# Latent-key attention: the causal mask added by VectorE in PSUM, in place of bf16 products of TensorE

## The chip, the core and the metric

The kernel runs on one core of a Trainium2 chip. It is written engine by engine: TensorE multiplies matrices into PSUM, VectorE and ScalarE read and write PSUM and SBUF, GpSimd works on SBUF, and semaphores order them. The metric is the device time of one execution in microseconds, the median of several runs.

## The reference

Eight layers are added one after another onto x of shape (4, 512, 256). Only the first concerns us, an attention with 16 heads and causal mask over 512 rows:

```python
q = (x @ wq).reshape(b, s, H, DN + DR)
q_nope, q_pe = (q[..., :DN], q[..., DN:])
q_pe = apply_rope(q_pe, cos, sin)
kv_a = x @ wkv_a
kv, k_pe = (kv_a[..., :R], kv_a[..., R:])
...
scores = jnp.einsum('bshd,bthd->bhst', qf, kf) * SCALE
mask = jnp.tril(jnp.ones((s, s), bool))
scores = jnp.where(mask[None, None], scores, jnp.finfo(scores.dtype).min)
p = jax.nn.softmax(scores, axis=-1)
out = jnp.einsum('bhst,bthd->bshd', p, v).reshape(b, s, H * DV)
return out @ wo
```

After it come a feed-forward layer, a cosine-similarity attention, the same feed-forward layer, a gated linear attention, a workspace layer, an attention with adapters and the workspace layer again.

## The kernel before

The latent-key attention is `mla_attention`. It folds the key weights into the queries, so that a head's key and query both have 128 rows (64 latent, 64 rotated). It loops over 32 pairs of heads, `n` = 0 to 31: 4 batches `b` of 8 pairs `p`. Head `j` of the pair is 0 or 1. The pairs are numbered 0 to 31 below.

There is no scheduler: each engine has its own list of calls, written out by hand, and semaphores between them. The scores of a head are a causal triangle of 128-wide tiles: tile row `qi` has (qi+1) x 128 columns. They lie in PSUM in `sc[:, j]`, three banks a head: row 3 in the first (512 columns), rows 2 and 0 in the second (384 + 128), row 1 in the third (256). `CAUSAL_ORDER` is 3, 2, 0, 1. `s_ready` counts finished banks.

The order of TensorE in pair n: `scores(n, 0)`, `spread_sums(n - 1)` (the reciprocal sums of the pair before, turned into `po`), `project(n + 1, 1)` (the rotated part of the next queries, into `pq`), `scores(n, 1)`, `attend(n - 1)` (probabilities times values, into `po`), `project(n + 1, 0)`, then `turn_probs` for both heads (ten transposes each), and pieces of row work for the next batch and the next layer ("lead" work), put in at certain pairs.

The order of VectorE: `maxima(n, 0)` (row maxima, negated, L535), `rope_queries(n + 1)`, `maxima(n, 1)`, `normalise(n - 1)` (onT), `copy_turned(n, 0)`, the reciprocal of the sums, `copy_turned(n, 1)`, and after that row and lead work, which stands ahead of `maxima(n + 1, 0)`.

The order of ScalarE: `exponents(n, 0)` (L681, for which it waits on `max_ready`), `copy_sums(n - 1)` (L674, `po` to `rb`), `exponents(n, 1)`, copies of the queries, and its share of the turned probabilities. `attend(n - 1)` waits for `r_copied`, that is for `copy_sums(n - 1)`; `turn_probs(n, j)` waits for the exponents of head j. GpSimd does the rotation (`rope`) and widens the reciprocal sums.

The mask on the diagonal tiles (0 below, -1e30 above the diagonal) is added by TensorE: behind each score product follows one of the identity with the mask tile, both in bf16, which accumulates into the diagonal tile (L792). float32 products show two passes in the trace, each with a weight load of its own.

Of the kernel before, what the change touches and what calls it, by code (L numbers as in the profile page):

```python
# [9 lines left out]
ALU = mybir.AluOpType  # L10
# [4 lines left out]
P = 128  # L15
B, S, D = 4, 512, 256
# [9 lines left out]
CAUSAL_COL = {3: 0, 2: S, 0: S + 3 * P, 1: 2 * S}  # L26
CAUSAL_COLS = 2 * S + 2 * P
CAUSAL_BANK = {3: 0, 2: 1, 0: 1, 1: 2}


class Kit:
# [339 lines left out]
def mla_attention(nc, g, w):  # L371


    with ExitStack() as ctx:
        k = Kit(nc, ctx)
        x, wap, wvo, ident, ident_b, mask_b = (g[n] for n in ("x", "wap", "wvo", "ident", "ident_b", "mask_b"))
# [13 lines left out]
        kT = k.sb("kT", [P, 2, 2, S])  # L390
        qT = k.sb("qT", [P, 2, 2, S])
# [30 lines left out]
        sc = k.ps("sc", [P, 2, 3 * 512])  # L422
# [16 lines left out]
        with nc.Block() as block:  # L439
# [15 lines left out]
            def _(dve):  # L455
# [74 lines left out]
                def maxima(n, j):  # L530
                    for qi in CAUSAL_ORDER:
                        if qi != 0:
                            dve.wait_ge(s["s_ready"], 6 * n + 3 * j + CAUSAL_BANK[qi] + 1)
                        at = CAUSAL_COL[qi]
                        red = dve.tensor_reduce(nmax[:, j, qi:qi + 1], sc[:, j, at:at + (qi + 1) * P],  # L535
                                                AX.X, ALU.max, negate=True)
                        if qi != 2:
                            red.then_inc(s["max_ready"], 1)
# [33 lines left out]
                for n in range(PAIRS):  # L572
                    b, p = divmod(n, MLA_PAIRS)
                    maxima(n, 0)
                    if n + 1 < PAIRS:
                        rope_queries(n + 1)
                    maxima(n, 1)
                    if n > 0:
                        normalise(n - 1)
                    copy_turned(n, 0)  # L580
                    if p == 6 and b + 1 < B:
                        scale_keys(b + 1)
                    dve.wait_ge(s["e_ready"], 6 * n + 6)
                    dve.reciprocal(rl[:, :, :], lsum[:, :, :]).then_inc(s["rl_ready"], 1)
                    copy_turned(n, 1)
                    if p == 0 and b > 0:
                        add_output(b - 1)
                    if b + 1 < B:
                        if p == 1:
                            row_stats(b + 1)  # L590
                        if p == 2:
                            norm_rows(b + 1)
                        if p == 5:
                            keys_values(b + 1, pq[:, :])
                    lead_vector(b, p)
# [52 lines left out]
            def _(act):  # L648
# [27 lines left out]
                def exponents(n, j):  # L676
                    for qi in CAUSAL_ORDER:
                        if qi != 0:
                            act.wait_ge(s["max_ready"], 6 * n + 3 * j + CAUSAL_BANK[qi] + 1)
                        at = CAUSAL_COL[qi]  # L680
# [40 lines left out]
            def _(pe):  # L721
# [57 lines left out]
                def scores(n, j):  # L779
                    b = n // MLA_PAIRS  # L780
                    if n > 0:
                        pe.wait_ge(s["pt_a"], 2 * (n - 1) + j + 1)
                        pe.wait_ge(s["pt_b"], 2 * (n - 1) + j + 1)
                    if j == 0:
                        pe.wait_ge(s["kT_ready"], 2 * b + 2)
                        pe.wait_ge(s["rope_done"], n + 1)
                        pe.wait_ge(s["qa_copied"], n + 1)
                    for qi in CAUSAL_ORDER:
                        at = CAUSAL_COL[qi]
                        pe.matmul(sc[:, j, at:at + (qi + 1) * P], qT[:, n % 2, j, qi * P:(qi + 1) * P],  # L790
                                  kT[:, b % 2, j, 0:(qi + 1) * P], start=True, stop=False)
                        last = pe.matmul(sc[:, j, at + qi * P:at + (qi + 1) * P], ident_b[:, :], mask_b[:, :],  # L792
                                         start=False, stop=True)
                        if qi != 2:
                            last.then_inc(s["s_ready"], 1)

# [62 lines left out]
                for n in range(PAIRS):  # L859
                    b, p = divmod(n, MLA_PAIRS)  # L860
                    scores(n, 0)
                    if n > 0:
                        spread_sums(n - 1)
                    if n + 1 < PAIRS:
                        pe.wait_ge(s["qa_copied"], n + 1)
                        if n > 0:
                            wait_for_piece(*divmod(n - 1, MLA_PAIRS))
                        project(n + 1, 1)
                    scores(n, 1)
                    if n > 0:  # L870
                        attend(n - 1)
# [2661 lines left out]
```

## Time and profile before

| What | us |
|---|---|
| median of 3 runs (2081.74 to 2083.86) | 2081.95 |
| the profiled execution | 2081.07 |
| its span, from the first to the last instruction | 2079.3 |
| TensorE busy in the span | 1938.0 (93%) |
| VectorE busy | 1018.0 (49%) |
| ScalarE busy | 807.5 (39%) |
| GpSimd busy | 519.2 (25%) |
| the latent-key attention, about | 37 to 559 |

Busy times are sums over instructions. A matmul's end is modelled, so the distance from one start to the next says more of TensorE's queue than the duration in a row. In a timeline row the time counts from the span's start, neighbouring instructions of a line are merged ("x4"), and a bracket gives the idle time before and what ended it. PE is TensorE's matmul, PEld its weight load, DVE VectorE, ACT ScalarE, POOL GpSimd.

### The profile page before, as it was taken

What the parts mean: (1) busy time and instruction counts of PE and PEld (TensorE: products, weight loads), DVE (VectorE), ACT (ScalarE), POOL (GpSimd) and SP (SyncE); (2) the same over time, 40 slices, a digit from 0 to 9 for tenths busy, and PEclk for the clock granted to TensorE, in tenths of its full rate; (3) what the DMA queues carried; (4) which work ended last, traced back from release to release, by engine and by line L of the source; (5) the groups of instructions that cost most, each with busy time, mean ns of one, the idle gap of its engine ahead of it and who ended that gap; (6) DMA issues with size and microseconds to landing.
All of it is one profiled execution on the core that took longest, in us unless ns stands there. A gap on an engine that the chain in (4) does not pass through costs nothing. (4 is left out here: it accounts for less than half of the span.)

```text
span 2079.3 us, 30272 instructions
## 1 busy us (share of the span) xinstructions
PE 1938.0 (93%) x11630; PEld 1249.0 (60%) x11630; DVE 1018.0 (49%) x2232; ACT 807.5 (39%) x1780; POOL 519.2 (25%) x621
## 2 busy tenths in 40 slices
PE   6999999999999999999999999978977799999876
PEld 4556656666666777677767766833255454545644
DVE  4554565546423234334333322288975565546444
ACT  2553544535433323332342334224424234445332
POOL 2322232223201111101110110045642243542222
PEclk9999999999999999999999999989999999999998
DMA  6000000000020000000000000020000000000001
GB/s 236 1 1 1 1 1 1 1 1 1 1 78 1 1 1 1 1 1 1 1 1 1 1 1 1 1 73 1 0 1 1 1 1 1 1 1 2 1 1 41
DMA packets 9773, 24.03 MB, mean 12 GB/s; under 512 B 2448, under 2 KB 6304, under 8 KB 8864
## 3 DMA queue, kind: packets, MB, share of 16 engines
q1 hardware_dynamic: 8336, 18.92, 2.5%
q10 hardware_dynamic: 1296, 3.18, 0.4%
q8 instruction: 94, 1.54, 0.3%
q14 instruction: 47, 0.39, 0.1%
HBM read 20.00 MB, written 2.10 MB: 11 GB/s over the span
## 5 line engine op out<-in xcount | busy, mean ns | idle before, releaser
L1512 PEld LDWEIGHTS cos_ps<-cos_vx,cos_probs 128*128 128x128 f32 x2048 | 239.0, 191 | 31.3 <-issue 30.1
L1512 PE MATMUL cos_ps<-cos_vx,cos_probs 128*128 128x129 f32 x2048 | 239.5, 275 | 1.0 <-DVE cos_on L1192 1.0
L1503 PE MATMUL cos_ps<-lead_room,cos_kT 128*128 128x512 f32 x512 | 230.7, 595 | 4.0 <-ACT lead_room L1355 2.4
L1384 ACT ACTIVATE cos_probs<-cos_ps 128x512 f32<-128x512 f32 x256 | 150.6, 597 | 165.1 <-PE cos_ps L1503 163.8
L681 ACT ACTIVATE probs<-sc,nmax 128x512 f32<-128x512 f32 (+3 forms) x256 | 132.3, 524 | 167.3 <-DVE nmax L535 165.2
L790 PE MATMUL sc<-kT,qT 128*128 128x512 f32 (+3 forms) x512 | 170.6, 455 | 3.9 <-DVE probsT L547 2.6
L1295 POOL TENSOR_TENSOR cos_qrs<-cos_qse,neg_half 128x4 f32<-128x4 f32 x59 | 59.4, 1007 | 443.8 <-DVE cos_qse L1174 443.8
L1503 PEld LDWEIGHTS cos_ps<-lead_room,cos_kT 128*128 128x128 f32 x512 | 94.6, 190 | 104.5 <-issue 98.4
L1172 DVE TENSOR_REDUCE cos_qss<-cos_qsq 128x4 f32<-128x512 f32 x59 | 40.4, 685 | 225.6 <-ACT cos_qsq L1363 225.6
L2988 DVE TENSOR_REDUCE cos_wq<-tail_ps 128x2 f32<-128x1024 f32 (+3 forms) x128 | 101.7, 823 | 81.0 <-PE tail_ps L3228 79.9
L762 PE MATMUL pq<-xnT,wap 128*128 128x512 f32 x256 | 125.5, 613 | 4.1 <-DVE swp L527 4.0
L535 DVE TENSOR_REDUCE nmax<-sc 128x1 f32<-128x512 f32 (+3 forms) x256 | 111.9, 483 | 27.8 <-PE sc L792 25.3
L3216 PE MATMUL tail_ps<-gla_vT 32*128 32x256 f32 (+3 forms) x512 | 105.9, 490 | 13.8 <-DVE cos_wq L2988 4.2
L790 PEld LDWEIGHTS sc<-kT,qT 128*128 128x128 f32 x512 | 80.5, 191 | 59.3 <-issue 58.1
L1534 PE MATMUL cos_ps<-cos_wout,cos_onT 128*128 128x256 f32 x512 | 115.7, 380 | 0.0
L3092 ACT ACTIVATE room<-tail_ps 128x768 f32<-128x768 f32 (+1 forms) x96 | 84.6, 881 | 68.7 <-PE tail_ps L3221 68.7
L1491 PE MATMUL cos_ps<-cos_wq,lead_room 128*128 128x512 f32 x236 | 111.1, 593 | 0.0
L615 POOL TENSOR_TENSOR rot<-swp,ropeT 128x512 f32<-128x512 f32 x32 | 40.6, 1267 | 271.7 <-DVE swp L527 271.7
L3221 PE MATMUL tail_ps<-gla_vT 32*128 32x256 f32 (+3 forms) x512 | 104.2, 485 | 0.0
L1534 PEld LDWEIGHTS cos_ps<-cos_wout,cos_onT 128*128 128x128 f32 x512 | 95.0, 190 | 11.7 <-issue 0.2
L1876 POOL TENSOR_TENSOR gla_qs<-gla_st,gla_qT 128x512 f32<-128x512 f32 x64 | 81.3, 1291 | 69.8 <-DVE gla_st L1751 69.8
L547 DVE COPY probsT<-sc 128x512 f32<-128x512 f32 (+1 forms) x128 | 65.3, 552 | 65.0 <-PE sc L804 65.0
(495 smaller groups left out, 3394.7 us busy)
## 6 DMA issues: line engine op xcount, KB each, us to landing
onT<-in_mla_wqT SPq DMA_DIRECT2D x1, 2048.0 KB, 9.5
lead_room<-in_mla_wo SPq DMA_DIRECT2D x1, 2048.0 KB, 19.8
cos_wq<-in_cos_wq SPq DMA_DIRECT2D x1, 2048.0 KB, 25.8
cos_wout<-in_cos_wout SPq DMA_DIRECT2D x1, 2048.0 KB, 7.6
out<-x SPq DMA_DIRECT2D x4, 512.0 KB, 2.9
x<-in_x SPq DMA_DIRECT2D x1, 1536.0 KB, 15.0
wq_pe<-in_mla_wq_pe ACTq DMA_DIRECT2D x1, 1024.0 KB, 14.6
x<-in_x SPq DMA_DIRECT2D x1, 512.0 KB, 4.6
```

Source lines behind the costliest of these rows:

```text
L535: red = dve.tensor_reduce(nmax[:, j, qi:qi + 1], sc[:, j, at:at + (qi + 1) * P], AX.X, ALU.max, negate=True)
L681: ex = act.activation(probs[:, j, at:at + (qi + 1) * P], sc[:, j, at:at + (qi + 1) * P], ACT.Exp, bias=nmax[:, j, qi:qi + 1], accum_out=ls ...
L762: last = pe.matmul(pq[:, :], wap[:, c, p, kind, :], xnT[:, b % 2, c, :], start=(c == 0), stop=(c == DC - 1))
L790: pe.matmul(sc[:, j, at:at + (qi + 1) * P], qT[:, n % 2, j, qi * P:(qi + 1) * P], kT[:, b % 2, j, 0:(qi + 1) * P], start=True, stop=False)
L1384: act.activation(probs[:, n % 2, kj, :], ps[:, kj, :], ACT.Exp).then_inc(s["e_done"], 1)
L1491: last = pe.matmul(ps[:, banks["project", b, u], :], xnT[:, b % 2, c, i * P:(i + 1) * P], wq[:, c, 512 * hq:512 * (hq + 1)], start=(c == 0 ...
L1503: pe.matmul(ps[:, kj, :], kT[:, b % 2, kj * P:(kj + 1) * P], qT[:, hq % 2, h % 4, :], start=True, stop=True).then_inc(s["s_ready"], 1)
L1512: last = pe.matmul(po[:, qi // 2, qi % 2, :], probs[:, n % 2, kj, qi * P:(qi + 1) * P], vx[:, b % 2, kj, :], start=(kj == 0), stop=(kj == ...
L1534: last = pe.matmul(y[i], onT[:, n % 2, a, :], wout[:, 8 * half + a, :], start=(half == 0 and a == 0), stop=(half == 1 and a == 7))
L2988: last = dve.tensor_reduce(qs[:, batch % 2, qi, h:h + 2, LORA_HD], ps[:, at:at + 2, col:col + n], AX.X, ALU.max, negate=True)
L3216: pe.matmul(ps[:, at + j, col:col + w], qT[r:r + LORA_SLOT, qi * P:(qi + 1) * P], kT[r:r + LORA_SLOT, n % 2, 0:w], start=True, stop=False)
L3221: turned = pe.matmul(ps[:, at + 2 + j, col:col + w], kT[r:r + LORA_SLOT, t % 2, kj * P:(kj + 1) * P], qT2[r:r + LORA_SLOT, kj * P:], start ...
```

## The change

The 256 mask products go (32 pairs, 2 heads, 4 tile rows). In `maxima`, VectorE waits for a bank as before, then adds the float32 mask tile to the bank's diagonal corner in PSUM, in place, drains, and then takes the maximum. The corners of rows 2 and 0 lie next to each other in the second bank, so one addition of 256 columns does both, and a head has three additions, of 128, 256 and 128 columns. ScalarE reads the masked scores after `max_ready` as before. A score product now closes its own accumulation and signals `s_ready`.

```diff
+CAUSAL_MASKS = ((S - P, P), (S + 2 * P, 2 * P), (2 * S + P, P))
...
                     for qi in CAUSAL_ORDER:
                         if qi != 0:
                             dve.wait_ge(s["s_ready"], 6 * n + 3 * j + CAUSAL_BANK[qi] + 1)
+                            at, width = CAUSAL_MASKS[CAUSAL_BANK[qi]]
+                            corner = sc[:, j, at:at + width].rearrange("p (n k) -> p n k", k=P)
+                            dve.tensor_tensor(corner, corner, g["mask"][:, :].unsqueeze(1).to_broadcast([P, width // P, P]),
+                                              ALU.add)
+                            dve.drain()
                         at = CAUSAL_COL[qi]
                         red = dve.tensor_reduce(nmax[:, j, qi:qi + 1], sc[:, j, at:at + (qi + 1) * P],
                                                 AX.X, ALU.max, negate=True)
...
                     for qi in CAUSAL_ORDER:
                         at = CAUSAL_COL[qi]
-                        pe.matmul(sc[:, j, at:at + (qi + 1) * P], qT[:, n % 2, j, qi * P:(qi + 1) * P],
-                                  kT[:, b % 2, j, 0:(qi + 1) * P], start=True, stop=False)
-                        last = pe.matmul(sc[:, j, at + qi * P:at + (qi + 1) * P], ident_b[:, :], mask_b[:, :],
-                                         start=False, stop=True)
+                        last = pe.matmul(sc[:, j, at:at + (qi + 1) * P], qT[:, n % 2, j, qi * P:(qi + 1) * P],
+                                         kT[:, b % 2, j, 0:(qi + 1) * P], start=True, stop=True)
                         if qi != 2:
                             last.then_inc(s["s_ready"], 1)
```

On TensorE, the queue from the scores of head 0 of pair 2 on stood so before (a row is a line, an operation, output<-inputs, its columns and what it waits for):

```order
L790 MATMUL sc<-kT,qT 128x512 [waits mla_rope_done,mla_kT_ready,mla_qa_copied,mla_pt_b,mla_pt_a]
L792 MATMUL sc<-mask_b,ident_b 128x128
L790 MATMUL sc<-kT,qT 128x384
L792 MATMUL sc<-mask_b,ident_b 128x128
L790 MATMUL sc<-kT,qT 128x128
L792 MATMUL sc<-mask_b,ident_b 128x128
L790 MATMUL sc<-kT,qT 128x256
L792 MATMUL sc<-mask_b,ident_b 128x128
L818 MATMUL po<-ident,rlw 128x128 [waits mla_o_done,mla_wvo_ready,mla_rl_wide]
L818 MATMUL po<-ident,rlw 128x128 x3
```

and stands so now, with the lines of the changed kernel:

```order
L798 MATMUL sc<-kT,qT 128x512 [waits mla_rope_done,mla_kT_ready,mla_qa_copied,mla_pt_b,mla_pt_a]
L798 MATMUL sc<-kT,qT 128x384
L798 MATMUL sc<-kT,qT 128x128
L798 MATMUL sc<-kT,qT 128x256
L824 MATMUL po<-ident,rlw 128x128 [waits mla_o_done,mla_wvo_ready,mla_rl_wide]
L824 MATMUL po<-ident,rlw 128x128 x3
```

Each score product now has the next one, with a weight load of its own, directly behind it.

On VectorE, the maxima of head 0 of pair 3 and what follows stood so before:

```order
L535 TENSOR_REDUCE nmax<-sc 128x1 [waits mla_s_ready] x2
L535 TENSOR_REDUCE nmax<-sc 128x1
L535 TENSOR_REDUCE nmax<-sc 128x1 [waits mla_s_ready]
L526 TENSOR_TENSOR rot1<-pq,ropeT 128x512 [waits mla_rope_done,mla_qb_ready]
L527 STREAM_SHUFFLE swp<-pq 128x512
```

and stand so now:

```order
L539 TENSOR_TENSOR sc<-sc,mask 128x128 [waits mla_s_ready]
L543 TENSOR_REDUCE nmax<-sc 128x1
L539 TENSOR_TENSOR sc<-sc,mask 128x256 [waits mla_s_ready]
L543 TENSOR_REDUCE nmax<-sc 128x1 x2
L539 TENSOR_TENSOR sc<-sc,mask 128x128 [waits mla_s_ready]
L543 TENSOR_REDUCE nmax<-sc 128x1
L529 TENSOR_TENSOR rot1<-pq,ropeT 128x512 [waits mla_rope_done,mla_qb_ready]
L530 STREAM_SHUFFLE swp<-pq 128x512
```

The wait for a bank moved from the maximum to the addition ahead of it, and the rotation input of the next pair stands behind three more operations.

## Rows read from the trace of the kernel before

**Rows 1.** Busy time of each engine in the stage, granted clock at the end.

```profile
37.00:555.00 518.00, 509.34 (x2688) 321.04 (x2688) 287.73 (x701) 251.56 (x714) 152.70 (x140) 1.00 0.00 1
```

**Rows 2.** Timeline, TensorE in pair 26: start, length, engine, line, operation, shapes, count.

```profile
470.91 1.02 PE L790 MATMUL sc<-kT,qT 128*128 128x512 f32 x2
...
473.46 0.61 PE L818 MATMUL po<-ident,rlw 128*128 128x128 f32 x4
...
475.63 1.02 PE L790 MATMUL sc<-kT,qT 128*128 128x512 f32 x2
...
476.48 0.22 PE L792 MATMUL sc<-mask_b,ident_b 128*128 128x128 bf16 x1
...
476.54 0.86 PE L790 MATMUL sc<-kT,qT 128*128 128x384 f32 x2
476.92 0.10 PEld L792 LDWEIGHTS sc<-mask_b,ident_b 128*128 128x128 bf16 x1
...
477.24 0.22 PE L792 MATMUL sc<-mask_b,ident_b 128*128 128x128 bf16 x1
...
478.27 2.37 PE L830 MATMUL po<-probsT,kc 128*64 128x512 f32 x16
...
482.39 2.35 PE L804 MATMUL sc<-ident,probs 128*128 128x128 f32 x20
...
484.57 0.60 PE L356 MATMUL pq<-cos_wq,lead_room 128*128 128x512 f32 x1
```

**Rows 3.** Timeline, VectorE and ScalarE in the same pair.

```profile
472.03 0.69 DVE L535 TENSOR_REDUCE nmax<-sc 128x1 f32<-128x512 f32 x1 [0.66 <-PE sc L792]
...
475.27 0.60 ACT L674 ACTIVATE rb<-po 128x512 f32<-128x512 f32 x1
...
477.06 1.85 DVE L535 TENSOR_REDUCE nmax<-sc 128x1 f32<-128x512 f32 x4
...
479.89 0.21 ACT L681 ACTIVATION_READ_ACCUMULATOR probs<-sc,nmax 128x1 f32 x1
```

**Rows 4.** Timeline, pair 14; in brackets the idle time before and its releaser.

```profile
257.28 1.02 PE L790 MATMUL sc<-kT,qT 128*128 128x512 f32 x2
...
262.62 1.68 DVE L535 TENSOR_REDUCE nmax<-sc 128x1 f32<-128x512 f32 x4
...
264.02 0.57 ACT L681 ACTIVATE probs<-sc,nmax 128x384 f32<-128x384 f32 x1
...
265.36 0.61 ACT L674 ACTIVATE rb<-po 128x512 f32<-128x512 f32 x1
...
266.02 2.16 PE L830 MATMUL po<-probsT,kc 128*64 128x512 f32 x12 [1.32 <-ACT rb L674]
```

**Rows 5.** Groups by line and shape of VectorE: count, busy us, mean ns, idle before.

```profile
L1744 DVE TENSOR_TENSOR gla_ps<-gla_ps,gla_kT 128x512 f32<-128x512 f32 x64 | 41.1, 687 | 6.7 <-PE gla_ps L2087 6.6
...
L535 DVE TENSOR_REDUCE nmax<-sc 128x1 f32<-128x384 f32 x64 | 35.6, 556 | 10.6 <-PE sc L792 8.1
...
L535 DVE TENSOR_REDUCE nmax<-sc 128x1 f32<-128x256 f32 x64 | 26.6, 415 | 0.0
...
L535 DVE TENSOR_REDUCE nmax<-sc 128x1 f32<-128x128 f32 x64 | 18.0, 281 | 0.0
```

**Rows 6.** Timeline of VectorE, four operations and the reduce behind a drain.

```profile
258.94 0.62 DVE L501 TENSOR_TENSOR kr<-kva,ropeN 128x64 f32<-128x64 f32 x4
259.65 0.42 DVE L504 TENSOR_REDUCE ss<-sq 128x4 f32<-128x256 f32 x1
```

**Rows 7.** Timeline, first scores and first maxima of pairs 6 and 18.

```profile
123.72 1.02 PE L790 MATMUL sc<-kT,qT 128*128 128x512 f32 x2
...
127.33 1.15 DVE L535 TENSOR_REDUCE nmax<-sc 128x1 f32<-128x512 f32 x2
...
331.51 1.10 PE L790 MATMUL sc<-kT,qT 128*128 128x512 f32 x2
...
335.96 1.15 DVE L535 TENSOR_REDUCE nmax<-sc 128x1 f32<-128x512 f32 x2
```

## The prediction

> **What bounds the kernel now.** I first take the busy time of the stage that the change touches, then one pair of heads in order of time, then the few pairs that look different. The stage is the latent-key attention, 37 to 555 us. TensorE is busy 509.34 of its 518 us, VectorE 287.73, at a granted clock of 1.00 [rows 1]. So TensorE's queue is the bound, and a product taken out of it is worth its issue time wherever no other engine takes over.
>
> A pair of heads shows how much room there is. In the pair that starts at 470.91 the steps of TensorE follow each other without a wait: scores of head 0 to 473.46, spread_sums and a projection to 475.63, scores of head 1 to 478.27, attend, a projection, and at 482.39 the 20 transposes of turn_probs, to 484.57 [rows 2]. The other engines are early: ScalarE starts the copy of the sums, for which attend waits, at 475.27 and needs some 0.65 us, so it is ready at about 475.9, 2.3 us before attend. The last exponent of head 1 is done at 480.10 (479.89 + 0.21); the transposes that need it are the second ten, at 482.39 + 1.09 = 483.48 [rows 2, 3]. That slack of 3.4 us repeats in 25 of the 32 pairs, with less only where VectorE comes late.
>
> I call D the time from a pair's first score pass to VectorE's first maximum. Here it is 472.03 - 470.91 = 1.12 us [rows 2, 3]. In six pairs VectorE still has row work (norms, keys, weights) in its queue, and D is large: 3.61 in pair 6 and 4.45 in pair 18 [rows 7], 5.34 in pair 14 [rows 4], and, read the same way, 3.00, 4.20 and 5.19 in pairs 9, 10 and 16. The other 26 lie between 1.1 and 1.9. In pair 14 the chain is visible: maxima at 262.62, second exponent at 264.02, copy of the sums at 265.36, attend at 266.02 after TensorE had waited 1.32 us [rows 4]. So attend can't start before D + 3.40 (266.02 - 262.62), against 7.36 after the pair's start in an undisturbed pair (478.27 - 470.91).
>
> **What the change removes.** 32 pairs x 2 heads x 4 tiles = 256 mask products. A product holds the queue 0.055 us (mask product at 476.48, next pass at 476.54, rounded to 0.01) [rows 2]. That is 14.1 us. It also exposes weight loads: the pass after it takes 0.38 us (476.54 to 476.92) where the second pass of the same shape takes 0.32 (476.92 to 477.24), since a product so short doesn't cover the float32 weight load behind it. Three of the four products of a head have such a pass behind them in the same call; the fourth shows no such excess. 192 x 0.06 = 11.5 us. Will the loads be hidden afterwards? The shortest float32 pass, of 128 columns, now stands in front of a load. The transposes are 20 such passes with a new load each, at (484.57 - 482.39)/20 = 0.109 us [rows 2], so yes. Together 25.6 us, 0.40 for a head, 0.80 for a pair. The call agrees: eight passes at 0.85 us for two of 512 columns (475.63 to 476.48), 0.64 for the two of 384, 0.43 for the two of 256 and 0.22 for the two of 128 make 2.14, and it takes 2.55 (470.91 to 473.46).
>
> The Trainium skill (TensorE: Matmul & The Clock Gate, "Back-to-back issue gap") gives about 81 ns per weight-load-and-matmul pair of 128 columns in a stream. By its figure, an estimate, the 256 products would be worth 20.7 us and the time would be some 5 us longer than mine. The rows here give 0.055 + 0.75 x 0.06 = 0.10 us, and I take them.
>
> **What it adds.** Three additions in PSUM for each head, of 128, 256 and 128 columns, each with a drain before its maximum. An addition with its input and output in PSUM is in the trace at 512 columns: 687 ns, while the maximum of 512 from PSUM into SBUF takes 690 [rows 3, 5]. So writing to PSUM costs nothing visible and I size the additions by the maxima of the same width: 281 ns at 128 and 415 at 256 [rows 5]. A drain costs the lost overlap and a gap: four operations end at 259.56, the reduce behind the drain starts at 259.65, so 0.08 us [rows 6], while without one neighbours overlap: the four maxima of 0.69, 0.556, 0.281 and 0.415 sum to 1.94 and take 1.68 together [rows 3 to 5], 0.09 for each seam. With back-to-back input the call takes 1.94 + 0.98 + 3 x 0.08 - 3 x 0.09 = 2.9 us in place of 1.68. Bounds for one added step on an extending chain: 0.28 (no drain cost) to 0.69 (the 512-column row).
>
> What waits for it? ScalarE's second exponent needs the maxima of tiles 2 and 0, after two additions: 0.28 + 0.08 + 0.69 - 0.09 + 0.415 + 0.08 + 0.556 - 0.09 + 0.28 = 2.20 us from the start of the call, and 0.05 to ScalarE. From the second exponent to attend it is 266.02 - 264.02 = 2.00 [rows 4]. So attend can't start before D + 4.25, against D + 3.40 before: 0.85 later. Undisturbed it now starts at 7.36 - 0.80 = 6.56.
>
> - *26 early pairs.* D + 4.25 is 5.4 to 6.2, under 6.56. Head 1: its scores start at 4.32 in place of 4.72, maxima 1.43 later (477.06 - 475.63) at 5.75, exponents done 2.20 + 0.05 + 1.47 = 3.7 after that, at 9.5. The second ten transposes come at 12.57 - 0.80 = 11.8 [rows 2, 3]. VectorE's additions are hidden by TensorE's own queue, with 2.3 us to spare there and 0.4 to 1.2 at attend. Behind the additions on VectorE stand the rotation input of the next pair (two operations for which GpSimd and the next projection wait) and then onT; onT's input is not there before attend ends. All 0.80 is kept. Were the cover gone, each pair would lose up to 2 x 1.2.
> - *Six late pairs.* New stall = D + 4.25 - 6.56, less the old one. Pair 6: 1.30. Pair 9: 0.69. Pairs 10, 14, 16 and 18 already stalled, so attend slips by 0.85 and the 0.80 is lost as well: 1.65 each. Sum 8.6 us. This wait takes the place of the one removed: attend on ScalarE's copy of the sums. Later waits in these pairs (transposes on exponents of head 1: in pair 14 done at 13.1, needed at 14.8) don't bind.
> - *First and last pair.* With a shorter queue they run into their exponent chain: about 0.3 and 0.45 us, 0.75 in all.
>
> **Sum.** -25.6 + 8.6 + 0.75 = -16.2 us. The profiled execution took 2081.07 us, 1.8 over its span, so 2064.9; the median of the runs shown, 2081.95, is 0.9 above it, so **2066**. The rest of the program comes after this stage and keeps its length. VectorE's total grows by some 64 x 1.2 = 77 us that nobody pays for outside the six pairs.
>
> **Rivals.**
> 1. *The weight loads stay exposed* (a stream of shorter passes pays its loads in another place). For: in the score call TensorE pays 0.06 for each today. Against: the transposes' 0.109. Then a pair gains 8 x 0.055 = 0.44, all pairs 14.1; the late pairs lose 4 x 1.3 + 0.95 + 0.35 = 6.5, the ends 0.5: 2075. With the Trainium skill's 81 ns a saving of 20.7 less some 8.5 of stalls and ends is 2070.
> 2. *The late pairs lose nothing*, because VectorE's row work itself starts earlier or attend has other cover: the full 25 us, 2057. Against: row work starts from the copies of the transposes, so it moves with the pair, and D stays.
> 3. *Slower: VectorE's chain of additions becomes the bound in every pair.* Place: attend in all pairs. It needs additions and drains in PSUM beside TensorE's writes to cost more than the rows say. With y more on the chain of two steps the six late pairs lose 6y, and the others what y exceeds their slack of 0.4 to 1.2. The 16.2 is used up at y = 1.4, so from 1.1 us for a step where I count 0.36 to 0.5. At 1.5 us a step (y = 2.1) it is some 36 us of loss: 2102. Against: 687 ns for 512 columns in PSUM while TensorE was at work.
>
> **How the numbers follow.** My forecast 0.73, its own range 2061 to 2071: the additions' bounds move six pairs by -0.2 to +0.5 each, slack that is thinner than counted in the three pairs with D near 1.9 adds 1, and the weight load behind each head's fourth product may turn out to be hidden too, 64 x 0.06, -4. Rival 1 0.14, rival 2 0.07, rival 3 0.06. The range 2060 to 2075 leaves rival 3 and most of rival 2 out. A change within 0.2%, 4 us, can't be told from none here: faster 0.91, same 0.04, slower 0.05.
>
> **What would show it.** In the profile after: in an undisturbed pair 2.15 us from the first score pass to spread_sums in place of 2.55, passes of one shape 0.32 and 0.32; 256 fewer products; the new additions at some 280 and 415 ns and a call of maxima of 2.9 us where its input is ready; TensorE's waits before attend for ScalarE's copy in the same six pairs, 0.7 to 3.0 us long, in total about 11.5 us (3.2 before). I am wrong if passes keep their 0.38, if attend waits in pairs with D under 2, or if an addition takes over 0.6 us.

## The result and the profile after

The changed kernel takes 2072.47 us, the median of four runs (2070.85 to 2074.29), and the kernel before 2082.44 on the same chip. The ratio is 0.9949 [0.9937, 0.9961]: 10.0 us faster, where 16.2 were forecast. The forecast was 2066 with a range of 2060 to 2075. One more run, at 2288.86 us with a mean granted clock of 0.838, is left out. Timed again later the kernel took 2072.62 against 2083.94, ratio 0.9945 [0.9932, 0.9958].

The page's head gives the totals. TensorE has 256 products fewer and 19 us less of busy time (1938.0 before), and VectorE has 60.7 us more (1018.0 before); the 77 of the forecast counted drains and lost overlap too, which busy time does not.

```profile
span 2070.2 us, 30144 instructions
...
PE 1918.8 (93%) x11374; PEld 1234.8 (60%) x11374; DVE 1078.7 (52%) x2424; ACT 809.6 (39%) x1780; POOL 520.9 (25%) x621
```

The table by windows of the stage answers to [rows 1]. VectorE is busy for 350.54 of 519 us, far from a bound, and TensorE for 497.94: it now idles 21 us, where it idled 9. The granted clock is 0.99 and no longer 1.00. Part of that small digit is what the forecast lacks.

```profile
35.00:554.00 519.00, 497.94 (x2474) 315.70 (x2475) 350.54 (x895) 254.51 (x716) 153.76 (x142) 0.99 0.00 1
```

The groups by line and shape answer to [rows 5]: count, busy us and mean ns of one, idle before. L539 is the new addition, L543 the maximum behind it, L836 attend.

```profile
L539 DVE TENSOR_TENSOR sc<-sc,mask 128x128 f32<-128x128 f32 x128 | 37.5, 293 | 16.3 <-PE sc L798 16.0
...
L539 DVE TENSOR_TENSOR sc<-sc,mask 128x256 f32<-128x256 f32 x64 | 27.1, 423 | 0.5 <-PE sc L798 0.5
...
L836 PE MATMUL po<-probsT,kc 128*64 128x512 f32 x128 | 35.8, 639 | 12.5 <-ACT rb L682 12.5
```

**An undisturbed pair.** TensorE's timeline of pair 26 answers to [rows 2]. Here all eight passes of a head stand in one row.

```profile
463.61 2.32 PE L798 MATMUL sc<-kT,qT 128*128 128x512 f32 x8
465.77 0.60 PE L824 MATMUL po<-ident,rlw 128*128 128x128 f32 x4
466.21 1.88 PE L770 MATMUL pq<-xnT,wap 128*128 128x512 f32 x4
467.93 2.32 PE L798 MATMUL sc<-kT,qT 128*128 128x512 f32 x8
470.18 2.38 PE L836 MATMUL po<-probsT,kc 128*64 128x512 f32 x16
472.49 1.98 PE L770 MATMUL pq<-xnT,wap 128*128 128x512 f32 x4
474.31 2.35 PE L810 MATMUL sc<-ident,probs 128*128 128x128 f32 x20
```

The score call takes 465.77 - 463.61 = 2.16 us in place of 2.55, so nothing is left of products or of exposed loads (the eight passes alone were 2.14). From the first scores to the second it is 4.32 in place of 4.72, and attend starts at 470.18 - 463.61 = 6.57 in place of 7.36. No row has a wait in brackets. The same pair on VectorE and ScalarE, against [rows 3]:

```profile
464.67 0.30 DVE L539 TENSOR_TENSOR sc<-sc,mask 128x128 f32<-128x128 f32 x1 [0.60 <-PE sc L798]
...
465.05 0.69 DVE L543 TENSOR_REDUCE nmax<-sc 128x1 f32<-128x512 f32 x1
465.66 0.42 DVE L539 TENSOR_TENSOR sc<-sc,mask 128x256 f32<-128x256 f32 x1
...
466.15 0.76 DVE L543 TENSOR_REDUCE nmax<-sc 128x1 f32<-128x384 f32 x2
...
466.82 0.29 DVE L539 TENSOR_TENSOR sc<-sc,mask 128x128 f32<-128x128 f32 x1
466.94 0.58 ACT L689 ACTIVATE probs<-sc,nmax 128x384 f32<-128x384 f32 x1 [0.39 <-DVE nmax L543]
467.19 0.42 DVE L543 TENSOR_REDUCE nmax<-sc 128x1 f32<-128x256 f32 x1
...
468.31 0.60 ACT L682 ACTIVATE rb<-po 128x512 f32<-128x512 f32 x1
```

A call of maxima lasts 467.61 - 464.67 = 2.94 us in place of 1.68. ScalarE is held up once inside its four exponents, for 0.39 us, by the maxima behind the second addition. It still ends the copy of the sums at 468.91, 1.3 us before attend. This is the hidden case.

**A late pair.** Pair 14, against [rows 4]. The first fence has TensorE, the second VectorE's first addition and two steps of ScalarE.

```profile
251.21 2.32 PE L798 MATMUL sc<-kT,qT 128*128 128x512 f32 x8
...
255.53 2.32 PE L798 MATMUL sc<-kT,qT 128*128 128x512 f32 x8
260.83 3.92 PE L836 MATMUL po<-probsT,kc 128*64 128x512 f32 x16 [2.98 <-ACT rb L682]
264.68 1.98 PE L770 MATMUL pq<-xnT,wap 128*128 128x512 f32 x4
```

```profile
256.55 0.29 DVE L539 TENSOR_TENSOR sc<-sc,mask 128x128 f32<-128x128 f32 x1
...
258.81 0.58 ACT L689 ACTIVATE probs<-sc,nmax 128x384 f32<-128x384 f32 x1 [0.39 <-DVE nmax L543]
...
260.17 0.60 ACT L682 ACTIVATE rb<-po 128x512 f32<-128x512 f32 x1
```

Attend starts 260.83 - 256.55 = 4.28 us after VectorE's first addition: the D + 4.25 of the forecast. The wait is 2.98 us. But the attend row is 3.92 us long, where an undisturbed one is 2.38, and nothing in the forecast asks for that. The table by windows has the reason in the column behind the engines, the granted clock: while attend runs its mean is 0.57, and in the stretch behind it 1.00 again.

```profile
260.83:264.48 3.65, 3.65 (x16) 1.46 (x16) 2.51 (x7) 2.02 (x7) 3.37 (x3) 0.57 0.03 7
264.50:268.00 3.50, 3.50 (x24) 2.32 (x20) 1.12 (x2) 1.48 (x5) 2.38 (x3) 1.00 0.00 0
```

A clock of 0.50 is the lower of its two levels, 1.2 GHz; before the change attend in this pair ran at 1.00 behind its wait of 1.32 us. Between attend's first and last pass there are 3.65 us; at full clock there are 2.10.

**All pairs.** This is each pair's length, from its first score pass to that of the next pair, worked out from the traces. The forecast column is the prediction's own terms.

```
pair                      before   after   diff   forecast
22 early ones, e.g. 17     13.67   12.89  -0.78   -0.80
0                          10.91   12.94  +2.03   -0.50   (11.31, +0.40, in two later traces)
6                          15.36   15.89  +0.53   +0.50
9                          13.67   13.60  -0.07   -0.11
10                         14.79   15.66  +0.87   +0.85
14                         16.74   19.16  +2.42   +0.85   attend at 0.57 of the clock
16                         28.72   31.28  +2.56   +0.85   attend at 0.58 of the clock
18                         15.02   15.89  +0.87   +0.85
27, 28              15.81, 14.10   15.35, 13.45   -0.46, -0.65   -0.80 each
first scores, pair 1 to 31: 496.89 -> 485.73 = -11.16     forecast 30 x -0.80 + 8.6 = -15.4
```

The span is 9.1 us shorter: -11.16 between pairs 1 and 31, +2.03 in pair 0, -1.63 ahead of it, and +1.6 from pair 31 to the end. Neither end is the change's as far as these traces tell. Pair 0 starts between 35.1 and 41.1 us over the 13 traces of this study. From pair 31 to the end, where the kernels differ in pair 31 alone, they take 1529.5 to 1540.2 us, and what varies with it is the granted clock: the trace with 1529.5 us spends 61 of them at the lower level, the two with 1539.6 and 1540.2 spend 89, and over all 13 the two quantities have a correlation of 0.91. The kernel before has such stretches there too, 78 us in its trace.

### The profile page after: what moved, and what is told of

It is laid out like the page before. It is cut to its first block and busy times, and to the rows that moved or that the text cites. A ratio compares the mean times of both kernels' runs of the same rounds, so it can differ in the third digit from the quotient of the medians.

```text
span 2070.2 us, 30144 instructions
## 1 busy us (share of the span) xinstructions
PE 1918.8 (93%) x11374; PEld 1234.8 (60%) x11374; DVE 1078.7 (52%) x2424; ACT 809.6 (39%) x1780; POOL 520.9 (25%) x621
## 5 line engine op out<-in xcount | busy, mean ns | idle before, releaser
L798 PE MATMUL sc<-kT,qT 128*128 128x512 f32 (+3 forms) x512 | 151.0, 438 | 4.3 <-DVE probsT L555 2.5
L798 PEld LDWEIGHTS sc<-kT,qT 128*128 128x128 f32 x512 | 86.1, 192 | 72.2 <-issue 54.4
L543 DVE TENSOR_REDUCE nmax<-sc 128x1 f32<-128x512 f32 (+3 forms) x256 | 119.8, 489 | 15.2 <-issue 1.4
```

What stands on the lines that cost most here:

```text
L798: last = pe.matmul(sc[:, j, at:at + (qi + 1) * P], qT[:, n % 2, j, qi * P:(qi + 1) * P], kT[:, b % 2, j, 0:(qi + 1) * P], start=True, stop ...
```

## The experiments

Two theories went in. **A**: everything is as forecast, and the missing 3.2 us in pairs 14 and 16 are the granted clock, which is at its lower level when attend restarts after a long wait. **B**: VectorE's additions write the score banks in PSUM while attend runs, and slow it. Behind them stand the three rivals of the prediction.

### 1. Only take the products out

VectorE's addition and its drain are left out of the changed kernel as well, so no mask is applied at all.

```
-  corner = sc[:, j, at:at + width].rearrange("p (n k) -> p n k", k=P)
-  dve.tensor_tensor(corner, corner, g["mask"]..., ALU.add)
-  dve.drain()
```

> The mask is left out altogether, on TensorE and on VectorE: the softmax also sees the keys above the diagonal of the diagonal tiles. It measures what the 256 products are worth with nothing in their place. Theory A (TensorE's queue is the bound, late pairs wait at attend for the chain of maxima, exponents and the copy of the sums, and after a wait of about 3 us the granted clock is at its lower level while attend runs, 1.6 us more): an undisturbed pair takes 0.78 us less, 25 us over 32 pairs; the chain is not longer than before, attend in the late pairs stays where it was, so five of them (6, 10, 14, 16, 18) give back 0.45 to 0.8 each, 3.5 in all. About 2061 us if the clock holds through waits of up to 2.2 us, 2063 to 2064 if it doesn't. Theory B (the additions in PSUM beside TensorE's writes slow TensorE down, so that attend took 3.9 us in pairs 14 and 16): 2061 us, attend 2.3 us long in every pair. A third: a shorter queue is worth less than its products because the whole program shifts; then less than 20 us.

Measured: 2063.04 us against 2081.48, ratio 0.991 [0.9888, 0.9933], -18.4. Early pairs lose the same 0.78 us as in the changed kernel. Pairs 10, 14, 16 and 18 are as long as before (14.79, 16.74, 28.71, 15.03), since their attend still waits for the same chain; pair 6 is at 15.01. In every pair attend has its 2.10 us from first to last pass. From pair 1 to pair 31 it is 477.38. What follows: the removal is worth 0.78 us a pair, and the additions take back 485.73 - 477.38 = 8.35 us of the loop in the late pairs, of which 3.2 is the clock. Pairs 27 and 28 take 15.35 and 13.44 here too, so their missing 0.3 and 0.1 us are not the additions' doing.

### 2. Only put the additions in

The products stay, and VectorE adds the mask as well; the mask is applied twice.

```
+BY_TENSOR = range(32)
...
+                        if n in BY_TENSOR:
+                            last = pe.matmul(sc[:, j, at + qi * P:at + (qi + 1) * P], ident_b[:, :], mask_b[:, :],
+                                             start=False, stop=True)
```

> The changed kernel with TensorE's products back in place: the mask is added twice, by TensorE and by VectorE. It measures VectorE's additions alone. Theory A: nothing in the 26 early pairs; attend moves 0.85 us later in pairs 10, 14, 16 and 18 and 0.5 in pair 6, 3.9 us in all, 2086.3 against 2082.4 before, with waits of 2.2 and 2.1 us in pairs 14 and 16; if such waits are already enough for the lower clock, 3.2 us more, 2089.5. Theory B (additions in PSUM slow TensorE): attend and the score calls are longer in pairs where additions lie beside them without any long wait ahead, and every early pair takes more than its 13.67 or 15.82 us.

Measured: 2089.75 against 2081.48, ratio 1.0032 [1.0018, 1.0046]. Early pairs from 1 on are as long as before to 0.03 us (13.67, 15.82), so the additions are free there. Pair 0 is not: 11.74 in place of 10.91, where nothing was expected. The loop from pair 1 to 31 is 5.6 us longer, 502.53: the expected 3.9 and some 1.6 more in pair 16. The late pairs give the clearest sight of the clock. TensorE's rows of attend in pair 14 and in pair 16:

```profile
272.55 2.38 PE L840 MATMUL po<-probsT,kc 128*64 128x512 f32 x16 [2.19 <-ACT rb L683]
...
305.12 3.35 PE L840 MATMUL po<-probsT,kc 128*64 128x512 f32 x16 [1.97 <-ACT rb L683]
```

Both waited for the same copy and have the same additions beside them. The one behind the longer wait runs in its usual 2.38 us, the other in 3.35. That already speaks against B, and also against any simple rule by which the length of the wait decides.

### 3. Products in pairs 14 and 16, additions elsewhere

The same switch with `BY_TENSOR = (14, 16)`, and VectorE's addition only `if n not in BY_TENSOR`.

> The changed kernel, but in pairs 14 and 16 the mask is added by TensorE's products again. Theory A: these two pairs go back to the 16.74 and 28.72 us of before, 2.42 and 2.56 less than in the changed kernel, and no stretch of the lower clock is left between pair 1 and the end of the stage: 2072.5 - 5 = 2067.5 us. Without the clock's part (attend 2.3 us whatever the wait) only 0.85 and 0.85 would come back: 2070.8. Theory B: as theory A in time, since the additions are gone too, so this run tells only the size.

Measured: 2075.9 against 2081.48, ratio 0.9967 [0.9952, 0.9981]. 2067.5 was expected, some 5 us below the changed kernel (0.9949 of before), and the median is not below it at all; the profiled execution took 2068.32. In its trace pairs 14 and 16 are 16.75 and 28.72 long, as expected, and then pair 18 is 17.88, where the changed kernel has 15.89:

```profile
332.62 1.94 PE L841 MATMUL po<-probsT,kc 128*64 128x512 f32 x4 [2.29 <-ACT rb L684]
```

Four passes take 1.94 us, where four take 1.08 in pair 16 of run 5 below. The lower clock is now behind the next long wait. Run 10, the same kernel again, has this wait of 2.29 us too, with attend in its usual 2.10 us and a pair of 16.18; so of the 17.88 the clock is 1.7, and 0.3 is a wait longer than the changed kernel's 2.00. The lower clock isn't tied to pairs 14 and 16. The median stayed unexplained, and I timed this kernel and the changed one again (runs 9 and 10).

### 4. Let ScalarE copy the sums first

Attend in the late pairs waits for ScalarE's copy of the sums of the pair before, which has its input early but stands behind four exponents that wait for VectorE. In the six late pairs the copy goes ahead of them.

```
+SUMS_FIRST = (6, 9, 10, 14, 16, 18)
...
+                    if n in SUMS_FIRST:
+                        copy_sums(n - 1)
                     exponents(n, 0)
-                    if n > 0:
+                    if n > 0 and n not in SUMS_FIRST:
                         copy_sums(n - 1)
```

> The changed kernel with one thing in another order: in the six late pairs (6, 9, 10, 14, 16, 18) ScalarE copies the sums of the pair before ahead of the exponents of head 0, so that attend no longer waits for VectorE's chain. The additions stay as they are. Theory A: attend starts at 6.6 us of the pair in all six and takes 2.3 us at the full clock; what is left is a wait of 0.3 to 1.8 us of the second ten transposes for the exponents of head 1 in pairs 10, 14, 16 and 18. Pairs 6, 9, 10, 14, 16, 18 take 1.3, 0.7, 1.6, 2.8, 3.3 and 1.6 us less: 2072.5 - 11.3 = 2061 us. Theory B (additions in PSUM slow TensorE): attend in pairs 14 and 16 still lies beside the additions of head 1 and still takes 3.9 us: 2064.5 us.

Measured: 2061.7 against 2081.48, ratio 0.99 [0.988, 0.992]. Attend starts 6.57 or 6.64 us after the pair's start in all six, with no wait, and has its 2.10 us. The pairs take 15.04, 12.89, 14.10, 16.74, 28.12 and 14.33, together 10.3 us less than in the changed kernel, where 11.3 was expected. Other waits come up behind attend: of the second ten transposes on exponents of head 1 (0.91 us in pair 14, 0.56 in pair 16, 0.29 in pair 18), of a projection on VectorE (0.63 in pair 14, 0.41 in pair 16), and in pairs 6 and 14 the wait for VectorE's keys that stands ahead of the next pair's scores grows (from 1.06 to 1.53 and 1.41). Pair 14 (246.88 to 263.62) has the most of them. The rows show VectorE's additions at 253.20 and 254.37, one running into attend's start and one in the midst of it:

```profile
253.20 0.42 DVE L540 TENSOR_TENSOR sc<-sc,mask 128x256 f32<-128x256 f32 x1
...
253.45 2.37 PE L839 MATMUL po<-probsT,kc 128*64 128x512 f32 x16
...
254.37 0.29 DVE L540 TENSOR_TENSOR sc<-sc,mask 128x128 f32<-128x128 f32 x1
...
256.45 1.98 PE L773 MATMUL pq<-xnT,wap 128*128 128x512 f32 x4 [0.63 <-DVE swp L531]
```

Attend takes 2.37 us with the additions beside it. That is the second piece of evidence against B. The projection then waits 0.63 us for VectorE, which is late itself.

### 5. The changed kernel, unaltered, once more

> The changed kernel once more, unaltered, for a second look at its trace. If the stretches of the lower clock follow from a wait alone, pairs 14 and 16 have attend at 3.6 to 3.7 us again and no other pair has it. If such a wait only makes the stretch possible, and it also depends on where the wait falls, other late pairs (10, 18) may show it this time and 14 or 16 not; the waits themselves are the same to 0.02 us (1.8, 3.1, 2.8 and 2.1 us in pairs 10, 14, 16 and 18).

Measured: one run, 2068.51 us. TensorE's rows of attend in pairs 14, 16 and 18, and under them the table by windows of the same three stretches:

```profile
264.02 1.68 PE L836 MATMUL po<-probsT,kc 128*64 128x512 f32 x6 [2.98 <-ACT rb L682]
...
297.46 1.08 PE L836 MATMUL po<-probsT,kc 128*64 128x512 f32 x4 [2.76 <-ACT rb L682]
...
339.19 1.10 PE L836 MATMUL po<-probsT,kc 128*64 128x512 f32 x4 [2.00 <-ACT rb L682]
```

```profile
264.02:267.60 3.58, 3.58 (x17) 1.52 (x17) 2.51 (x7) 1.94 (x7) 3.29 (x3) 0.64 0.03 7
297.46:299.70 2.24, 2.24 (x16) 1.06 (x16) 2.09 (x6) 0.96 (x3) 2.10 (x2) 1.00 0.00 0
339.19:342.60 3.41, 3.41 (x16) 1.51 (x16) 2.51 (x7) 2.13 (x8) 3.12 (x3) 0.63 0.00 0
```

The waits are those of the first trace to 0.01 us. The lower clock is not: it is in pairs 14 and 18 now, and pair 16, with its 2.76 us of wait, runs at 1.00. In pair 18 the first four passes still go at the usual speed (1.10 us) and the clock falls behind them. The same program with the same waits gets it in other places. From pair 1 to 31 it is 485.78 all the same, since two pairs pay in either trace. Pair 0 is 11.31 long, and its first scores run at full clock: in the first trace the lower level reached into it (0.50 from 35.40 to 37.50, and the score call takes 3.87 us in place of 2.16).

### 6. Longer waits without any addition

The kernel before, with its products. In pairs 10, 14, 16 and 18 VectorE takes the first maximum of head 0 three times, each extra one with a drain, so that attend waits about as long as in the changed kernel, and nothing writes the score banks but TensorE.

```
+                        if n in (10, 14, 16, 18) and j == 0 and qi == 3:
+                            for _ in range(2):
+                                dve.tensor_reduce(nmax[:, j, qi:qi + 1], ..., AX.X, ALU.max, negate=True)
+                                dve.drain()
```

> The kernel before, with TensorE's mask products and no addition in PSUM; in pairs 10, 14, 16 and 18 VectorE takes the first maximum of head 0 two extra times, each with a drain. This makes the chain 1.54 us longer there and TensorE's wait at attend 1.7, 2.9, 2.8 and 2.0 us, near those of the changed kernel. Theory A (a long wait is followed by the lower clock): 6.2 us more than before for the waits, and attend takes some 3.6 us in place of 2.1 in one to three of the four pairs, 1.6 us each: 2089 to 2093 us against 2082. Theory B (the additions in PSUM slow attend): attend takes 2.1 us in all four pairs, 2088 us.

Measured: 2090.73 against 2081.39, ratio 1.0047 [1.0031, 1.0063]. Attend in pairs 14 and 16, and the window of pair 14:

```profile
267.86 1.97 PE L835 MATMUL po<-probsT,kc 128*64 128x512 f32 x4 [2.85 <-ACT rb L679]
...
302.87 2.37 PE L835 MATMUL po<-probsT,kc 128*64 128x512 f32 x16 [3.01 <-ACT rb L679]
```

```profile
267.86:271.40 3.54, 3.54 (x16) 1.41 (x16) 1.08 (x4) 2.14 (x8) 3.26 (x3) 0.60 0.02 5
```

The total is as theory A had it (2089 to 2093), and so is pair 14: the lower clock behind a wait of 2.85 us, with no addition in the program. B falls. Pair 16 has none behind 3.01 us. So a wait of this size is followed by the lower level in some places and not in others.

### 7. The copy first, in the kernel before

The order of run 4 on ScalarE, with the products of before.

> The kernel before, mask products on TensorE, with the order of the run sums_first on ScalarE: the copy of the sums ahead of the exponents of head 0 in pairs 6, 9, 10, 14, 16 and 18. It tells how much of the gain of sums_first is the order alone. Theory A: only the waits of before go away, 0.2, 1.4, 1.2 and 0.4 us in pairs 10, 14, 16 and 18: 3.2 us less than before, 2079. If the order were worth the same here as in the changed kernel, it would be some 10 us less, 2072.

Measured: 2079.75 against 2081.39, ratio 0.9994 [0.9981, 1.0007]: the total can't be told from no change. In the trace the loop from pair 1 to 31 is 493.86, 3.03 shorter than before (expected: 3.2). Pairs 10, 14, 16 and 18 are 14.61, 15.52, 27.55 and 14.61 long. The change of place is thus worth 3.0 us to the kernel before and 485.73 - 475.47 = 10.3 us to the changed one. The mask's move alone shortens the loop by 11.2 us, the order alone by 3.0, and both together by 21.4: the order lets the late pairs keep what the shorter queue saves.

### 8. Copy first, products kept in pairs 0 and 14

> The kernel of sums_first, and in pairs 0 and 14 the mask is added by TensorE again. In pair 0 there is no attend ahead of the transposes, so TensorE waits for the exponents of head 1, and the additions cost more than the products: 0.41 us back. In pair 14 the chain of head 1 is what is left: by theory A it takes 16.74 - 1.39 = 15.35 us in place of 16.74. Together 1.8 us less than sums_first, 2060 us. If it isn't less, the additions were not what those two pairs waited for.

Measured: 2064.0 against 2081.39, ratio 0.9914 [0.99, 0.9927]. 2060 was expected. Pair 14 gets shorter by 1.23 us (15.51, expected 15.35), and the loop from 1 to 31 by 0.99 (474.48), since pair 18 is 0.29 longer. Whether pair 0 got back its 0.41 us this trace can't say: it is 13.09 long, since the lower clock covers its start. No gain over run 4 shows in the total; the rest of the program took 1538.5 us from pair 31 in this trace and 1534.0 in that of run 4, more than what is looked for.

### 9 to 11. The changed kernel, 14/16 and the copy first, together on one chip

> The changed kernel, unaltered, timed on the same chip as the next two. By the theory as it stands (25 us from the products, less the waits, less 1.6 us for each stretch of the lower clock that falls on a late pair): 2070 to 2073 us, with stretches of the lower clock after one to three of the waits in pairs 10, 14, 16 and 18.

> The mask by TensorE in pairs 14 and 16 alone, once more: its trace gave what was expected (2068.3 us, both pairs back at 16.75 and 28.72) and the median of its runs did not (2075.9). If that was where the lower clock falls from run to run, it now lies 2 to 5 us under the changed kernel on the same chip. If this kernel is really slower than its trace, it lies above the changed kernel again, and the reason isn't in the two pairs.

> The additions everywhere and the copy of the sums first in the six late pairs, once more, on the same chip: 9 to 11 us under the changed kernel, 2060 to 2062, attend 2.1 us long in every pair. If the first result was chance, the distance is under 5 us.

```
                              median us (lowest, highest)   ratio to before [95%]      pairs 1 to 31
before                        2083.94 (2081.49, 2086.19)
changed kernel                2072.62 (2071.43, 2074.91)    0.9945 [0.9932, 0.9958]    485.70
products in 14 and 16         2071.78 (2069.65, 2079.71)    0.995  [0.9934, 0.9966]    481.03
copy of the sums first        2063.18 (2060.31, 2066.33)    0.9899 [0.9886, 0.9912]    475.46
```

Copy first is 9.4 us under the changed kernel, as expected. The kernel with the products in 14 and 16 is 4.7 us shorter in the loop in these traces, and 0.8 in the medians, where 2 to 5 were expected; that is no difference here. Its runs spread over 10 us; its first trace had the lower clock in pair 18, and this one has it nowhere in the loop. So the gain in two pairs is shown by the trace and by no total. This second trace of the changed kernel has the lower clock in pairs 14 and 16 again (3.61 and 3.66 us in attend), not in 18.

## Why the prediction came out as it did

The time came out inside the stated range and outside the 2061 to 2071 that the prediction gave its own mechanism: 10.0 us of gain, where 16.2 were forecast. The wide range, not the sum, took in what was overlooked.

**What bounds the kernel, and what the removal is worth: right.** TensorE's queue was the bound. A pair lost 0.78 us where 0.80 was forecast, in the changed kernel and with nothing in the products' place (run 1). Both parts of it were needed: the score call fell to 2.16 us, the sum of its passes, so the float32 weight loads are hidden, as the transposes' 0.109 us had said. Rival 1 falls. A product with what it exposed cost 0.39 / 4 = 0.098 us; by rows of before it was 0.10. The Trainium skill (TensorE: Matmul & The Clock Gate, "Back-to-back issue gap") has 81 ns for a load and matmul of 128 columns in a stream; four of these are 0.32 us, so the trace doesn't bear it out between float32 passes: 0.07 of the measured 0.39 are missing.

**What the additions cost: right.** 293 and 423 ns against 281 and 415, and 2.94 us for a call against 2.9. A neighbour by shape (the 512-column addition in PSUM), scaled by the maxima of the right widths, was enough. That the early pairs hide them was right too: those of the changed kernel are as long as those of run 1, where no addition is, to 0.03 us. So rival 3, in which the additions bound every pair, falls.

**Where they are paid: right in place and mechanism.** In the six late pairs and nowhere else in pairs 1 to 30, attend waits on ScalarE's copy of the sums:

```profile
PE po L836 <- ACT rb L682: 12.5, 8, 3.0
```

The row has two waits more than the six: 0.42 in pair 31, which the forecast had at 0.45, and 0.69 behind the loop. The six are 1.25, 0.64, 1.77, 2.98, 2.76 and 2.00, in sum 11.4; before, four of these pairs waited, 2.9 in all. The forecast said 11.5 and 3.2, a slip: its own terms add up to 11.9 and 3.3. They are the better number. Counted by how far attend starts behind its place in an undisturbed pair (6.57 us now, 7.35 before), the six are 12.0 late and were 3.4 late, 8.7 more for a term of 8.6. Run 2 shows the cause alone, and run 4 removes it by the order of ScalarE alone. Rival 2 falls.

**The step that was mis-sized: "Six late pairs. ... 1.65 each. Sum 8.6 us".** Read from the lengths of the six pairs it is 7.18 + 6 x 0.78 = 11.86. In pairs 14 and 16 attend then ran at the lower level of the clock and took 1.55 and 1.53 us longer; the two pairs are 1.55 and 1.69 above the 0.87 that pairs 10 and 18 show, 3.2 us. Without it the term is 8.6. The prediction had put nothing in the sum for it: it took the granted clock of 1.00 from before as given. The forecast priced a wait at its length. Here a wait of 2 to 3 us cost, in two of the three longest cases, over half its length again. Before the change the longest wait at attend was 1.3 us and none was followed by it. Runs 5, 6 and 2 show that it goes with the waits and not with the additions, and that it moves between pairs 14, 16 and 18 from one execution to the next. With the waits gone (runs 4, 7, 8 and 11) no trace has it between pairs 1 and 31. What decides which wait gets it stays open; the longest wait of all in these traces, 3.01 us, didn't.

**Smaller terms.** Pair 0 was to give back 0.5 us and instead cost 0.4. With the shorter queue its second ten transposes wait 0.53 us for exponents of head 1, of which I had counted about 0.3, and then the scores of pair 1 wait 0.39 for ScalarE's copy of the turned probabilities, which stands behind its copies of the queries. From start to start the two cost 0.7 and 0.6 us. That second wait I had not looked for. In the first trace of the changed kernel, whose rows these are, the lower clock at the pair's start adds 1.6 more.

```profile
46.64 1.31 PE L810 MATMUL sc<-ident,probs 128*128 128x128 f32 x10 [0.53 <-ACT probs L689]
48.34 1.12 PE L798 MATMUL sc<-kT,qT 128*128 128x512 f32 x2 [0.39 <-ACT probsT L696]
```

Pairs 27 and 28 gave 0.3 and 0.1 us less than the others, also without any addition (run 1). There `spread_sums` writes into the `po` bank that ScalarE still copies out for the next layer:

```profile
480.40 0.60 ACT L304 ACTIVATE lead_room<-po 128x512 f32<-128x512 f32 x1
...
481.10 0.63 PE L824 MATMUL po<-ident,rlw 128*128 128x128 f32 x4
```

The copy ends at 481.00, and `spread_sums` starts 2.45 us after the pair's start (478.65) in place of 2.16; in pair 28 the copy ends at 496.17 and it starts at 496.26. Before the change the longer score call, 2.55 us, covered this. The 0.78 in place of 0.80 makes the rest. In sum: 16.2 - 3.2 (clock) - 0.9 (pair 0) - 0.9 (early pairs) = 11.2 against 10.0 by the first medians and 11.3 by the second. The 1.2 between is less than the rest of the program varies by from trace to trace.

**A better version.** The order of run 4 with the products out takes 2061.7 and 2063.2 us in two timings, 0.990 of before, against 0.9945 for the change alone.

## What to carry to other kernels

When work moves from the bounding engine to one with time to spare, do the sum twice: for the queue that gets shorter, and for the few places where the other engine is already late, since there the engine pays the added chain and loses the saving too. Then look at what the waiting instruction really needs: here it was a copy whose input was long there, behind four exponents that waited for VectorE, and moving it ahead was worth about as much as the change itself. Price a new wait of some us with the clock that may follow it, and judge such parts by the length of each stage in the trace, since a total that varies by 3 us or more from run to run hides them.

## What the runs showed of the hardware that I had not expected

- The granted clock fell to its lower level at some of TensorE's waits of 2 to 3 us (2.98, 2.85, 2.76, 2.29, 2.00, 1.97) and not at others (3.01, 2.76, 2.29, 2.19, 2.10, 2.00), with the same program and waits equal to 0.01 us in two executions. Over all traces the loop has 16 waits of 1.97 us or more at attend; 9 of them had it, and no shorter one. The fall came between 0.56 us before attend's start, within the wait, and 1.24 us after that start. Attend then took 2.93 to 3.79 us from first to last pass in place of 2.10.
- An addition with its input and output in PSUM and a mask in SBUF, beside TensorE at work: 293 ns at 128 columns, 423 at 256.
- Between an addition and the maximum behind its drain VectorE stands 0.07 or 0.08 us in 189 of 192 cases of the changed kernel's trace, and 0.42 to 0.50 in the other three, put down to "issue". In pair 14:

```profile
262.45 0.76 DVE L543 TENSOR_REDUCE nmax<-sc 128x1 f32<-128x384 f32 x2 [0.42 <-issue]
```
